# Retention layer with a quantised FFN: the old state read in two 64-row halves, the output projection moved into a score bank, and the root chain behind the masked scores

## What is computed

```python
# attention part, B=2, L=2048, 256 features, 8 heads, 32 columns of q and k and 64 of v a head
qkv = hidden_states @ w_qkv.T
q, k = _xpos(q, k)
dm = where(causal, decay ** (t - s), 0)
retention = einsum('bhtd,bhsd->bhts', q, k) * scale * dm
out = einsum('bhts,bhsv->bhtv', retention, v)
normed = (out - mu) / sqrt(var + EPS)             # over the 64 columns of a head
y = silu(hidden_states @ w_gated.T) * normed @ w_proj.T
x = layernorm(x + y)
# FFN part, every operand quantised to FP4 in blocks of 16 and scaled back
h = silu(fp4(x) @ fp4(w_gate).T) * (fp4(x) @ fp4(w_up).T)
x = layernorm(x + fp4(h) @ fp4(w_down).T)
```

## Time and profile before

| | us |
|---|---|
| median of 3 runs | 629.73 (629.08 to 630.48) |
| the profiled execution | 630.59 |
| its span in the trace | 628.4 |
| TensorE matmul busy | 586.9 (93%) |
| VectorE busy | 536.8 (85%) |
| ScalarE busy | 337.1 (54%) |
| GpSimd busy | 228.9 (36%) |

### The profile page before, as it was taken

How to read it: one execution, slowest core, us unless ns; L and a number is a source line. 1 busy time by engine, 2 the same in 40 slices (tenths; PEclk the granted TensorE clock), 3 DMA queues, 4 the chain that set the end, 5 groups by cost and what they waited for, 6 DMA issues and landing times.

```text
span 628.4 us, 14613 instructions
## 1 busy us (share of the span) xinstructions
PE 586.9 (93%) x4304; PEld 499.8 (80%) x4304; DVE 536.8 (85%) x1433; ACT 337.1 (54%) x868; POOL 228.9 (36%) x260
## 2 busy tenths in 40 slices
PE   7999999999999999999998696959999999999975
PEld 3788888888878887878887575858999888888864
DVE  6667788889888988898897857879999999999996
ACT  3356575666667676757676553424444444444433
POOL 2111123343434343434333205444444545444530
PEclk9999999999999999999999989887999999999998
DMA  7610111011101100110110000000000000000001
GB/s 207 199 44 10 51 52 43 10 50 50 31 19 50 50 23 27 50 42 9 49 33 18 9 10 1 0 2 17 19 17 17 27 23 17 17 17 17 17 18 51
DMA packets 24955, 22.15 MB, mean 35 GB/s; under 512 B 2009, under 2 KB 21858, under 8 KB 24930
## 3 DMA queue, kind: packets, MB, share of 16 engines
q1 hardware_dynamic: 24114, 20.27, 10.6%
q10 hardware_dynamic: 816, 1.57, 0.7%
HBM read 17.63 MB, written 4.20 MB: 35 GB/s over the span
## 4 chain that ended last, share of the span: by engine, by line
DVE 33%; issue 22%; PE 19%; ACT 13%; POOL 9%; DVEq 2%; DMA 2%; ACTq 1%; POOLq 0%
PE wide_banks L1213 8%; ACT shared L444 5%; POOL shared L1182 4%; POOL shared L1187 3%; PE mixed L1276 3%; DVE shared L801 3%; DVE shared L806 2%; PE upd_y L1213 2%; DVE h_amax L786 2%; ACT shared L459 2%; PE mixed L1269 2%; ACT squares L436 2%; DVE shared L1001 2%; DVE shared L997 2%; DVE stats L640 2%
## 5 line engine op out<-in xcount | busy, mean ns | idle before, releaser
L1187 POOL TENSOR_TENSOR shared<-shared,h_scale 128x704 f32<-128x704 bf16 x32 | 44.5, 1390 | 92.5 <-DVE shared L806 92.5
L1213 PE MATMUL wide_banks<-wgu_hi,xq_hi 128*128 128x512 f32 (+1 forms) x192 | 63.4, 413 | 10.8 <-DVE xq_lo L990 10.8
L444 ACT ACTIVATE shared<-opened,rstd 128x64 f32<-128x64 f32 x256 | 64.7, 335 | 13.3 <-DVE rstd L719 13.0
L415 ACT ACTIVATE shared<-shared 128x704 bf16<-128x704 f32 x32 | 25.3, 791 | 84.4 <-POOL shared L1182 84.4
L1213 PE MATMUL wide_banks<-win_hi,x_hi 128*128 128x512 f32 x192 | 67.8, 434 | 0.5 <-DVE shared L629 0.4
L1276 PEld LDWEIGHTS mixed<-shared 128*128 128x128 f32 x512 | 62.0, 192 | 2.8
L1182 POOL TENSOR_TENSOR shared<-shared,h_inv 128x704 f32<-128x704 f32 x32 | 44.6, 1392 | 50.7 <-DVE h_inv L797 50.7
L1276 PE MATMUL mixed<-shared 128*128 128x64 f32 x512 | 60.6, 271 | 0.0
L1213 PE MATMUL wide_banks<-win_hi,x_lo 128*128 128x512 f32 x192 | 60.4, 396 | 0.0
L1213 PE MATMUL wide_banks<-win_lo,x_hi 128*128 128x512 f32 x192 | 60.3, 395 | 0.0
L1138 POOL TENSOR_TENSOR x_lo<-xf,x_hi 128x256 fp32r<-128x256 f32 x32 | 23.3, 728 | 99.3 <-DVE rsq L704 49.8
(11 more groups left out here) (153 smaller groups left out, 1490.6 us busy)
## 6 DMA issues: line engine op xcount, KB each, us to landing
xf<-in_x_feat SPq DMA_DIRECT2D x32, 128.0 KB, 2.2
tab<-in_tables SPq DMA_DIRECT2D x16, 256.0 KB, 2.7
xt<-in_x_tok SPq DMA_DIRECT2D x32, 128.0 KB, 2.1
out<-shared SPq DMA_DIRECT2D x32, 128.0 KB, 1.7
x<-in_w_in ACTq DMA_DIRECT2D x3, 512.0 KB, 5.5
w<-in_w_gu SPq DMA_DIRECT2D x1, 1408.0 KB, 8.2
w<-in_w_down SPq DMA_DIRECT2D x1, 704.0 KB, 9.4
wgu_lo<-pow_dram SPq DMA_DIRECT2D x1, 576.0 KB, 4.7
```

The costliest lines, as they stand in the source:

```text
L415: act.activation(h_size[:, b], h_unit[:, b], ACT.Abs, scale=SIZE_BY).then_inc(h_fp4["rounder_ready"], 1)
L444: last = act.activation(gated[:, b, cols], opened[:, b, cols], ACT.Copy, scale=rstd[:, b, 1 + k:2 + k])
L1187: pool.tensor_tensor(over_blocks(hq[:, b]), over_blocks(h_steps[:, b]), spread(h_fp4["scale"][:, b]), ALU.mult).then_inc(h_fp4["ready"], 1)
L1213: last = pe.matmul(dst, lhs, rhs, start=k == 0, stop=k == len(parts) - 1)
```

## The change

- The PSUM tensors are laid out anew. `mixed` is now the upper halves (columns 256 to 511) of two banks, one for each pair of heads of a group; `upd` is in the lower half of the second of these. `y` moves to the upper half of the second score bank; for the last three tiles it is in the lower half of bank 6 (`y_of`).
- `cross` reads the state in row halves of 64: four products with 64 rows and 128 columns, the halves going to different banks. `state_bd` shrinks from 2 x 2 x 256 to 2 x 2 x 128 columns.
- Because banks are shared in a new way, waits move: `scores` waits for `resid_done` of tile n - 4; `update` waits for `opened_ready`; `upd_done` is raised by the last product of `cross`, no longer of `update`; `mix` waits for `state_summed`; `project_out` waits for `ret_ready` where it waited for `state_summed`.
- On VectorE, `decay_scores` goes ahead of the four root steps square, product, fine and fine square, in even tiles. Square and product now follow it, fine follows `split_gated`, and fine square follows `sum_state`. GpSimd's hold (`behind_queries`) ends with `decay_q`.
- The rest follows from the new order of heads: `place`, strided reads in `apply_gate` and `square_heads`, `wproj` loaded by two DMAs in place of one. The FFN's output banks (`z_of`) are the lower halves of banks 5 and 6.

```diff
-        wide_banks = psum("wide_banks", [P, 5, BANK])
+        wide_banks = psum("wide_banks", [P, 7, BANK])
         proj, score = wide_banks[:, 0:3], wide_banks[:, 3:5]
-        mixed = psum("mixed", [P, BANK])
-        upd_y = psum("upd_y", [P, GROUPS * DV + DM])
-        upd = upd_y[:, 0:GROUPS * DV].rearrange("p (g v) -> p g v", v=DV)
-        y = upd_y[:, GROUPS * DV:]
+        mixed = wide_banks[:, 5:7, DM:BANK]
+        y = score[:, 1, DM:BANK]
+        upd = wide_banks[:, 6, 0:GROUPS * DV].rearrange("p (g v) -> p g v", v=DV)
...
-            sp.dma_start(wproj[:], w_proj.rearrange("(c p) n -> p c n", p=P)).then_inc(ld_proj, 16)
+            for r in range(2):
+                sp.dma_start(wproj[:, 2 * r:2 * r + 2], w_proj.rearrange("(g r p) n -> r p g n", g=GROUPS, p=P)[r]).then_inc(ld_proj, 16)
...
-                dve.tensor_tensor(opened[:, b], mixed[:], gate[:, b], ALU.mult).then_inc(opened_ready, 1)
+                dve.tensor_tensor(opened[:, b].rearrange("p (r g c) -> p r g c", r=2, g=GROUPS), mixed.rearrange("p r (g c) -> p r g c", g=GROUPS),
+                                  gate[:, b].rearrange("p (g r c) -> p r g c", g=GROUPS, r=2), ALU.mult).then_inc(opened_ready, 1)
...
                 if valid(n):
                     decay_q(n)
+                if valid(n):
+                    decay_scores(n)
                 if joint:
                     joint_square(n)
                     joint_product(n)
-                    joint_fine(n)
-                    joint_fine_square(n)
-                if valid(n):
-                    decay_scores(n)
...
                 if in_turn(n - LAG):
                     split_gated(n - LAG)
+                if joint:
+                    joint_fine(n)
...
                 if carried(n):
                     sum_state(n, b)
                 if joint:
+                    joint_fine_square(n)
                     joint_fine_product(n)
...
                 need(pe, ret_ready, n)
+                need(pe, resid_done, n - LAG)
...
                 for g in range(GROUPS):
-                    pe.matmul(mixed[:, PER * DV * g:PER * DV * (g + 1)], qdT[:, g], state_bd[:, b, g],
-                              start=g == 0, stop=False, skip_group_check=True)
+                    for r in range(2):
+                        rows = slice(2 * DQ * r, 2 * DQ * (r + 1))
+                        last = pe.matmul(mixed[:, r, 2 * DV * g:2 * DV * (g + 1)], qdT[rows, g], state_bd[rows, b, g],
+                                         start=g == 0, stop=False, skip_group_check=True)
+                if carried(n):
+                    last.then_inc(upd_done, 1)
...
                 pe.wait_ge(ret_ready, n + 1)
+                if carried(n):
+                    pe.wait_ge(state_summed, n + 1)
...
                 need(pe, state_summed, n)
-                need(pe, resid_done, n - LAG)
+                need(pe, opened_ready, n)
...
-                last.then_inc(upd_done, 1)
...
-                pe.wait_ge(state_summed, n + LAG + 1 if not isinstance(n, int) else min(n + LAG + 1, TILES - BATCH))
-                accumulate(y, [(t[:, P * c:P * (c + 1)], w[:, c]) for t, w in
+                if isinstance(n, int) and n >= TILES - LAG:
+                    pe.wait_ge(opened_ready, TILES)
+                else:
+                    pe.wait_ge(ret_ready, n + LAG + 1)
+                accumulate(y_of(n), [(t[:, P * c:P * (c + 1)], w[:, c]) for t, w in
```

More of the change, by code:

```diff
@@ L81, in slot, with place @@
     return 2 * (h % PER) + h // PER
+def place(h):
+    g, j = divmod(h, PER)
+    return PER * (j // 2) + 2 * g + j % 2
 def retention_ffn(nc, x_tok, x_feat, w_in, w_proj, w_gu, w_down, decay, tables, eye, pow_dram, out):
@@ L246, in retention_ffn @@
         W_PARTS = [range(0, 3), range(3, 5), range(5, W_GROUPS)]
+        halves = lambda t: t.rearrange("p (r c) -> p r c", r=2)
         head_cols = lambda t: t.rearrange("p (h v) -> p h v", v=DV)
@@ L291, in weights, with y_of @@
             return W_PARTS[part] if isinstance(n, int) and n == TILES - 1 else ()
+        def y_of(n):
+            return wide_banks[:, 6, 0:DM] if isinstance(n, int) and n >= TILES - LAG else y
         def resid2_of(n, b):
@@ L435, in square_heads @@
                 need(act, heads_summed, n)
-                act.activation(squares[:], mixed[:], ACT.Square, scale=DV ** -0.5).then_inc(squared, 1)
+                act.activation(halves(squares[:]), mixed, ACT.Square, scale=DV ** -0.5).then_inc(squared, 1)
             def normalise_heads(n, b):
@@ L458, in place_state @@
                     rows = slice(DQ * j, DQ * (j + 1))
-                    last = act.activation(state_bd[rows, b, :, DV * j:DV * (j + 1)], state[rows, b], ACT.Copy)
+                    last = act.activation(state_bd[rows, b, :, DV * (j % 2):DV * (j % 2 + 1)], state[rows, b], ACT.Copy)
                 last.then_inc(state_placed, 1)
@@ L635, in add_resid @@
                 need(dve, x1_ready, n - 1)
-                dve.tensor_tensor(resid[:, b], y, xt[:, b], ALU.add).then_inc(resid_done, 1)
+                dve.tensor_tensor(resid[:, b], y_of(n), xt[:, b], ALU.add).then_inc(resid_done, 1)
             def resid_stats(n, b):
@@ L1268, in cross @@
                 for g in range(GROUPS):
-                    pe.matmul(mixed[:, PER * DV * g:PER * DV * (g + 1)], qdT[:, g], state_bd[:, b, g],
-                              start=g == 0, stop=False, skip_group_check=True)
+                    for r in range(2):
[4 more added lines that the diff above has]
+                    last.then_inc(upd_done, 1)
             def mix(n, b):
                 pe.wait_ge(ret_ready, n + 1)
+                if carried(n):
+                    pe.wait_ge(state_summed, n + 1)
                 for k in range(HEADS):
-                    last = pe.matmul(mixed[:, DV * k:DV * (k + 1)], ret[:, slot(k)], vs[:, b, DV * k:DV * (k + 1)],
-                                     start=False, stop=k == HEADS - 1, skip_group_check=True)
+                    r, at = place(k) // PER, place(k) % PER
+                    last = pe.matmul(mixed[:, r, DV * at:DV * (at + 1)], ret[:, slot(k)], vs[:, b, DV * k:DV * (k + 1)],
+                                     start=False, stop=k >= HEADS - 2, skip_group_check=True)
                 last.then_inc(out_done, 1)
@@ L1288, in update @@
                         k = PER * g + j
-                        last = pe.matmul(upd[DQ * j:DQ * (j + 1), g], kd[:, DQ * k:DQ * (k + 1)], vs[:, b, DV * k:DV * (k + 1)],
-                                         start=True, stop=True)
-                last.then_inc(upd_done, 1)
+                        pe.matmul(upd[DQ * j:DQ * (j + 1), g], kd[:, DQ * k:DQ * (k + 1)], vs[:, b, DV * k:DV * (k + 1)],
+                                  start=True, stop=True)
             def turn_gated(n, b):
@@ L1350, in _ @@
             for _ in range(WARM):
-                pe.matmul(turn[:], state_bd[:, 0, 0, 0:P], state_bd[:, 0].rearrange("p g v -> p (g v)"), start=True, stop=True)
+                pe.matmul(turn[:], state_bd[:, 0, 0], state_bd[:].rearrange("p b g v -> p (b g v)"), start=True, stop=True)
             def turn_weights(group):
```

12 lines of the change are left out of this document (6 added, 6 removed).

## The result

| | before | after |
|---|---|---|
| median, beside each other | 629.23 (628.98 to 630.48) | 633.14 (632.81 to 634.44) |
| ratio | | 1.0054, interval 1.0041 to 1.0067 |
| the profiled execution | 630.59 | 633.1 |
| its span | 628.4 | 631.0 |

The changed kernel is 0.54% slower. The forecast was 0.3% faster, and the result is outside its range (625.9 to 630.6).

The account below looks back on a forecast made before the run. TensorE's chain was taken to bound tiles 0 to 7 and the end of attention, VectorE's and ScalarE's the loop. 1.84 - 0.45 + 0.20 + 0.26 = 1.85 us less gave 627.9 us (chance 0.42), range 625.9 to 630.6.

Parts of the forecast that it names:

- In the loop: Tiles 8 to 29, on VectorE's and ScalarE's chain: -0.02 us a pair (-0.09 to +0.06), 0.2 us less over ten pairs.
- The rest, costed at nothing: Side effects taken as 0: shorter clearing of `state_bd`, strided reads, GpSimd's split of x in even tiles, second `wproj` DMA.
- the third rival: Halves don't overlap; VectorE waits for scores in even tiles: 635.3 us, or 632.3 with a saving near zero; chance 0.12.
- cross in row halves: TensorE's `cross` takes 0.67 us as four rounds like `scores`, 2.14 to `mix`: 0.23 us less in each tile.
- Tiles 0 to 7: Ahead of the loop, wholly on TensorE's chain: 8 x 0.23 = 1.84 us less.
- The start: Shorter clearing of `state_bd` halves at the head of the table of powers: counted 0, upper end 0.45 us.
- Tile 8: Where the chain goes from TensorE to VectorE: later root steps give 0.45 us back.
- Behind the loop: Tile 30, chain back on TensorE: `project_v` follows the shorter `cross`, 0.26 us less; tile 31 nothing.
- The strided reads: `apply_gate` and squares read in pieces: counted 0; at 0.02 us each, 20 tiles would give back 0.8 us.
- the first rival: Halves give more, by full overlap (0.43 us a tile) and shorter start: 625.0 us, half the extras 626.3; chance 0.18.

Follow-up runs that it names:

- run 5: Kernel before with only the new order of the root chain and its even-tile hold of GpSimd, no change of banks or halves: 632.40 us, ratio 1.0036.
- run 1: Changed kernel with GpSimd's split of x also waiting for `decay_q` in odd tiles: 629.14 us, ratio 0.998.
- run 4: Changed kernel with the old order of the root chain and old even-tile hold, new banks and halves kept: 627.89 us, ratio 0.9965; repeated unchanged, 628.64 us, 0.9968.
- run 9: Changed kernel with GpSimd's split of x held in odd tiles too, and the eight records of `cross` on all 128 rows: 632.58 us, ratio 1.0044.
- run 2: Kernel before with GpSimd's split of x held behind `decay_q` in odd tiles, nothing else: 629.63 us, ratio 1.0002.
- run 7: Changed kernel, GpSimd not held, `w_scale` and `w_inv` moved from the odd tile's start to the even tile's end, behind `sum_squares`: 629.53 us, ratio 0.9988.
- run 6: Changed kernel, not held, with GpSimd's split of x in odd tiles issued as two pieces of 128x128: 630.15 us, ratio 1.0002.
- run 3: Kernel before with ScalarE's `split_x` ahead of `open_gate` in odd tiles, so GpSimd's split of x is released earlier: 634.28 us, ratio 1.0079.

## Why the prediction was wrong

**The step that failed** is "In the loop", -0.02 us a pair, which measured +0.47. The term that it lacked is the wait of `w_inv` for GpSimd's split of x.

- *"The rest, costed at nothing"* had GpSimd's split of x in even tiles only, and there it looked for what stands beside it. The odd tile's split was not looked at, since no line of the change touches it. It is released by ScalarE and ScalarE by TensorE, and I had myself put TensorE 0.23 us ahead and VectorE 0.06 late, 0.29 together. The earlier trace rows begins with the scores, too late to show that 0.29 us were all that lay between the starts of `w_inv` and of the split. The measured shift is some 0.36 (from about 1.83 to 2.19, run 5). The rule of the Trainium skill cited above is on just this case. The collision cost 0.46 us a pair, 4.6 us in ten (run 1 against the change), and it was not among the rivals either.
- *The rest of the step* was right. Without the collision (run 1) the pair is 21.42 against 21.41: the even tile takes 9.78 to 9.79 in place of 9.70 (forecast 0.06 more), the odd one 11.63 in place of 11.71 (forecast up to 0.09 less). The order of the root chain is that cheap only with the halves. Alone it costs 0.21 a pair (run 5), by VectorE's wait for the scores, which the third rival had priced at 0.25. That wait shrinks with what `cross` saves, but does not go: with 0.22 saved it is still 0.12 to 0.14 in even tiles, where my sum had next to none.

**cross in row halves**: right, except where the masked scores still release `project_v` (2.62 us to `mix` in tiles 0 to 2 as before, 2.41 in run 4's even loop tiles). Elsewhere 2.15 us to `mix` against 2.14, and run 9 shows the overlap to be its reason. My reason for 0.67 (four rounds, as in `scores`) measured 0.64.

**Tiles 0 to 7**, 1.84 us: mechanism right, size off. From the first transposes of tile 3 to those of tile 7 the distances are 10.33, 10.30, 10.29 and 10.28 in place of 10.56, 10.56, 10.56 and 10.66. But from tile 0 to tile 3 nothing is gained: 8.76, 8.89 and 8.79 in place of 8.75, 8.79 and 8.79. There is no `turn_gated` in them, and `project_v` waits for the masked scores after `cross` is done:

```profile
20.22 1.23 DVE L640 TENSOR_TENSOR shared<-wide_banks,shared 128x1024 f32<-128x1024 f32 x1 [1.03 <-PE wide_banks L1274]
20.44 0.71 PE L1285 MATMUL wide_banks<-shared,qdT 64*128 64x128 f32 x8
21.59 0.71 PE L1226 MATMUL wide_banks<-win_hi,x_hi 128*128 128x512 f32 x2 [0.43 <-DVE shared L640]
```

I had given that very release to tile 31 and not to the first three. From 93.8 to 92.3 us, with the old order, the halves give 1.5 ahead of the loop. The start, bounded at 0.45, gives nothing: the clearing is 0.43 us shorter, and the first transposes come at 17.14 us both in run 2 (with the long clearing) and in run 4 (with the short one).

**Tile 8**, 0.45 back for the root chain: 92.9 with the new order against 92.3 with the old one, 0.6. A little more.

**Behind the loop**, 0.26: more, 0.54. To the end of the span nothing can be read, since the stretch from the last weight step varies from 302.1 to 303.4 us between two traces of the same kernel (run 4 and its repeat). But up to the last `apply_gate` it is steady: 27.04 before and in run 2, 27.00 and 27.01 with the halves alone (run 4 and its repeat), 26.75 with the new order alone (run 5), 26.50 after the change. So the new order gives 0.29, and the halves 0.25 only behind it.

**The strided reads**, bounded at 0.8: nothing. `apply_gate` takes 692 ns in both, ScalarE's squares 578 ns against 580.

**The rivals.** The third named the right mechanism for slower at the right place, with 632.3 where the halves save nothing; runs 5 and 9 are that case and measured 632.4 and 632.6. In the changed kernel it was not what happened, since the halves do save 0.22. Its span of times (632.3 to 635.3) has the result in it, by another cause; that is luck. In the first rival, half of the way is 626.5 by its own terms, not 626.3, and the loop's chain holds two thirds of the attention phase (22 of 32 tiles), not three quarters; neither matters here. In the traces the changed kernel has 0.7 us less up to the first weight step, 4.7 more in the loop and 1.5 less behind it, of which 0.5 are those above and the rest is within what that stretch varies by: 2.5 more in all (2.6 between the spans). Between the medians it is 3.9.

Where the border lies, the first pairs of the loop show. A scaling operation that starts within 0.01 us of the split isn't held (`w_scale` in the changed kernel, `x_inv` in run 7), with one exception (`w_scale`, once in run 6, 0.48 us). One that starts 0.02 us behind is held to the split's end, as these two lines of run 3 show, and one 0.03 behind (`x_scales` in run 7) as well:

```profile
109.89 0.73 POOL L1140 TENSOR_TENSOR x_lo<-xf,x_hi 128x256 fp32r<-128x256 f32 x1 [2.07 <-ACT x_hi L396]
109.91 0.73 DVE L770 TENSOR_SCALAR w_scale<-w_amax 128x24 f32<-128x24 f32 x1
```

What stays open: whether the split would wait the other way round. In run 5 it starts 0.03 us behind the start of `w_inv` and takes 0.73, as ever.

## What to carry to other kernels

When a change moves one engine against another, list the operations of VectorE and GpSimd that run within half a microsecond of each other, the ones that the edit doesn't touch too, and write down the distance. A distance smaller than the shift is a term of the sum. A small operation's median duration, not its count, shows the hold. And test the parts of a change alone: here the good part (0.3%) was hidden by one that undid it.

## What the runs showed that I had not expected

- A VectorE operation of 24 numbers a row waits for a GpSimd subtraction of 0.76 us to end: 0.70 instead of 0.17. RECIPROCAL beside the same split isn't held (0.35 and 0.24 in run 5, and the same in run 1, where it doesn't run beside it), nor is `decay_q`, which has an input in PSUM (0.36 in the kernel before, beside the split, and in run 1, not beside it). TENSOR_SCALAR from SBUF to SBUF is. Every held one ends 0.03 to 0.04 us behind the operation that holds it.
- Four records in one half of the rows, issued one after another, and then four in the other take no longer than eight in turn: 0.65 us either way. Their records start in pairs either way.
- Eight records of 128 columns take nearly as long as four of 256 on all rows: 2.40 and 2.37 us from the first to `mix`, in tile 4.
